# Windowed attention and a routed expert layer: score rows by (chunk, query), one product block a group, and another order of the eight-step pipeline

## The reference

```python
x = x + attention(layernorm_over_channels(x))   # 8x8 windows, 4 heads of 16, table bias
t = tokens(x)                                   # (4, 16384, 64)
t = t + experts(layernorm(t))                   # 8 experts, the best 2 of a softmax router
# attention, for each window and head:
attn = softmax(q @ k.T * hd**-0.5 + bias[rel_index])    # 64 x 64
out  = attn @ v ;  out = out @ w_proj.T + b_proj
# experts: sum over the two chosen e of p_e * (x @ W_e + b_e)
```

## Time and profile before

| what | value |
|---|---|
| median of 3 runs | 1214.26 us (1211.23 to 1214.93) |
| the profiled execution | 1211.91 us, span 1210.1 us |
| TensorE matmul busy | 1081.3 us, 89% |
| VectorE / ScalarE / GpSimd busy | 904.1 / 742.7 / 475.6 us (75 / 61 / 39%) |
| mean granted TensorE clock | 0.983 of full speed |

### The profile page before, as it was taken

One profiled execution on the slowest core, in us unless ns is written; L12 is line 12 of the kernel. 1 busy time (PEld: TensorE's weight loads), 2 busy tenths in 40 slices (PEclk: granted clock), 3 DMA queues, 4 the chain that ended last, 5 costly groups with the idle time before them and its releaser, 6 DMA issues.

```text
span 1210.1 us, 39081 instructions
## 1 busy us (share of the span) xinstructions
PE 1081.3 (89%) x16838; PEld 591.3 (49%) x16838; DVE 904.1 (75%) x1443; ACT 742.7 (61%) x1217; POOL 475.6 (39%) x421
## 2 busy tenths in 40 slices
PE   1688899999999999999999999999999999999653
PEld 1355455555555455555555555555555555554311
DVE  3246788888778788888778888888778888788552
ACT  0257767666766667666766667666766667665410
POOL 0001434444344434444344434444344434444443
PEclk9999999999999999999999999999999999999877
DMA  5000787666766887666667887666677887666667
GB/s 179 2 2 22 175 196 176 164 162 168 173 165 169 191 195 179 162 161 170 169 163 172 193 196 170 165 161 167 167 175 171 193 194 168 166 161 149 146 148 162
DMA packets 49255, 192.48 MB, mean 159 GB/s; under 512 B 10558, under 2 KB 10814, under 8 KB 32572
## 3 DMA queue, kind: packets, MB, share of 16 engines
q1 hardware_dynamic: 49084, 189.98, 65.6%
HBM read 154.04 MB, written 18.87 MB: 143 GB/s over the span
## 4 chain that ended last, share of the span: by engine, by line
PE 56%; DVE 19%; POOL 10%; ACT 7%; issue 3%; DMA 3%; SPq 1%; POOLq 0%; DVEq 0%; ACTq 0%
PE bank L594 10%; POOL tt L886 9%; PE bank L477 7%; PE bank L510 6%; PE bank L465 5%; PE bank L527 5%; PE bank L534 4%; PE bank L492 3%; DVE L L1109 3%; DVE ob L1067 3%; ACT prj L769 3%; PE bank L438 3%; ACT sq L775 3%; DVE Ls L1108 3%; PE bank L553 3%
## 5 line engine op out<-in xcount | busy, mean ns | idle before, releaser
L914 POOL TENSOR_TENSOR gz<-gz,tt 128x1024 f32<-128x1024 f32 x96 | 262.8, 2737 | 170.9 <-DMA gz<-gates_dram 170.9
L594 PE MATMUL bank<-gz,wex 64*64 64x512 f32 x2048 | 265.5, 614 | 16.2 <-DVE ob L1067 14.5
L886 POOL TENSOR_TENSOR tt<-prj,xs 128x512 f32<-128x512 f32 x64 | 109.1, 1727 | 369.1 <-ACT prj L769 369.1
L1036 DVE TENSOR_REDUCE mx<-bank 128x16 f32<-128x1024 f32 x128 | 156.1, 1220 | 106.5 <-PE bank L477 106.5
L1058 DVE TENSOR_TENSOR gz<-gz,tt 128x1024 f32<-128x1024 f32 x160 | 212.9, 1333 | 28.3 <-DMA gz<-gates_dram 28.3
L752 ACT ACTIVATE pt<-bank 128x512 f32<-128x512 f32 x256 | 151.2, 590 | 35.0 <-PE bank L510 34.2
L477 PE MATMUL bank<-km,qs 32*64 32x128 f32 x4096 | 172.5, 283 | 0.2
L510 PE MATMUL bank<-cst,probs 128*128 128x128 f32 x1024 | 167.5, 286 | 2.1 <-ACT pt L752 2.1
L1043 DVE TENSOR_TENSOR probs<-bank,mx 128x1024 f32<-128x1024 f32 x128 | 156.2, 1220 | 7.3 <-PE bank L510 1.8
L510 PEld LDWEIGHTS bank<-cst,probs 128*128 128x128 f32 x1024 | 110.3, 141 | 93.4 <-issue 58.9
L477 PEld LDWEIGHTS bank<-km,qs 32*64 32x64 f32 x4096 | 109.9, 132 | 67.1 <-issue 63.3
(11 more groups left out here) (111 smaller groups left out, 1432.1 us busy)
## 6 DMA issues: line engine op xcount, KB each, us to landing
gz<-gates_dram SPq DMA_DIRECT2D x256, 512.0 KB, 11.6
xs<-in_x SPq DMA_DIRECT2D x32, 512.0 KB, 16.3
tx<-tt SPq DMA_DIRECT2D x128, 128.0 KB, 3.9
out<-ob SPq DMA_DIRECT2D x128, 128.0 KB, 4.8
gz<-in_rel SPq DMA_DIRECT2D x1, 2048.0 KB, 9.4
gates_dram<-gt_rs SPq DMA_DIRECT2D x32, 64.0 KB
cst<-in_consts SPq DMA_DIRECT2D x1, 359.0 KB, 3.0
tt<-in_weights SPq DMA_DIRECT2D x4, 64.0 KB, 2.7
```

The lines of the kernel that those rows point to most:

```text
L594: last = mm(bank[64 * x:64 * x + 64, Y_BANK + a, :], wex[64 * a:64 * a + 64, e, :], gz[64 * a:64 * a + 64, s.pair(e)[1], e % 2, x * CH:(x ...
L886: tt_(chunk_windows(tt[s.buf(4)], x), as_windows(prj[:, x, :]), chunk_windows(xs[s.buf(4)], x), op=ALU.add).then_inc(t_ready, 1)
L914: tt_(gz[:, k, e % 2, :], gz[:, k, e % 2, :], tt[s.buf(4)][:, :], op=ALU.mult).then_inc(z_pool, 1)
L1036: red(mx[g % 2][:, :], two_banks(S_BANK).rearrange("p (c k) -> p c k", k=N), axis=AX_X, op=ALU.max).then_inc(max_done, 1)
```

## The change

It does four things.

1. Scores are laid out by (chunk, query) in the partitions; all four windows i of a group's chunk lie along the free dimension. The row tiles of chunk 0 write partitions 0 to 63 and those of chunk 1 partitions 64 to 127 of the same bank. `scores_left`, `scores_right` and `s_half` become one `scores`, with bias and all 16 products of a group in one block and no wait inside. `probs` and `pt` change shape to suit (the number and size of all instructions stay; `denominators` reads `pt` in runs of 64 elements in place of 128).
2. LAST_STAGE is 7: 39 steps. `project`, `move_proj`, `residual`, `square_residual` and `router` move from s3 to s4, most `experts` from s5 to s6 and the last three to s7, `finish` and `store` to s7, `swap_tokens` and the first three `spread_gates` to s5, and the loading and squaring of x to s0.
3. All five lists have another order.
4. `ROUNDS` is reordered to match.

```diff
-    LAST_STAGE = 6
+    LAST_STAGE = 7
...
-            0: [("lgT", 4, L_ready, 2), ("K", 2, k_ready, 2), ("Q", 2, q_ready, 1), ("stats", 1, var_done, 1),
-                ("gT", 4, gsb_ready, 2), ("V", 2, v_ready, 2), ("proj", 3, prj_ready, 1), ("spread", 1, xr_ready, 1)],
-            1: [("K", 2, k_ready, 2), ("Q", 2, q_ready, 1), ("V", 2, v_ready, 2), ("proj", 3, prj_ready, 1),
-                ("spread", 1, xr_ready, 1), ("router", 3, lg_ready, 1)],
+            0: [("proj", 4, prj_ready, 1), ("Q", 2, q_ready, 1), ("stats", 1, var_done, 1),
+                ("lgT", 4, L_ready, 2), ("K", 2, k_ready, 2), ("spread", 1, xr_ready, 1), ("gT", 4, gsb_ready, 2),
+                ("V", 2, v_ready, 2)],
+            1: [("proj", 4, prj_ready, 1), ("Q", 2, q_ready, 1), ("router", 4, lg_ready, 1), ("K", 2, k_ready, 2),
+                ("spread", 1, xr_ready, 1), ("V", 2, v_ready, 2)],
...
-                score_tiles(s, g, 0).then_inc(s_half, 1)
-
-            def scores_right(s, g):
-                pe.wait_ge(s_half, s.count(GROUPS, g + 1))
-                score_tiles(s, g, 1).then_inc(s_full, 1)
+                a = g // 2
+                for i in range(4):
+                    w = 4 * (g % 2) + i
+                    for r in range(4):
+                        x, hp = r // 2, r % 2
+                        last = mm(bank[N * x:N * x + N, S_BANK + hp, 128 * i:128 * i + 128],
+                                  qs[32 * r:32 * r + 32, a, w, :],
+                                  km[32 * r:32 * r + 32, CW * a + w, :, :].rearrange("p m k -> p (m k)"),
+                                  start=False, stop=(i == 3), skip_group_check=True)
+                last.then_inc(s_full, 1)
...
-                for r in range(4):
-                    last = nc.tensor.transpose(bank[:, PT_BANK, 128 * r:128 * r + 128],
-                                               probs[g % 2][:, r % 2, r // 2, u % 2, :], cv("ident"))
+                for j in range(2):
+                    for hp in range(2):
+                        at = 128 * (2 * j + hp)
+                        last = nc.tensor.transpose(bank[:, PT_BANK, at:at + 128],
+                                                   probs[g % 2][:, hp, 2 * (u % 2) + j, :], cv("ident"))
```

More of the change, by code:

```diff
@@ L602, in _ @@
                 if s[3].on:
-                    transposes(s[3], 3)
+                    transposes(s[3], 2)
+                if s[4].on:
+                    project(st, s[4])
+                if s[7].on:
+                    experts(s[7], 5)
+                    experts(s[7], 6)
+                if s[2].on:
+                    queries(st, s[2])
+                if s[3].on:
+                    transposes(s[3], 3)
+                if s[7].on:
+                    experts(s[7], 7)
+                if s[1].on:
+                    channel_sums(st, s[1])
+                if s[3].on:
+                    values(s[3], 0)
+                    values(s[3], 1)
+                if s[4].on:
+                    router(st, s[4])
+                if s[3].on:
+                    denominators(s[3], 0)
+                    transposes(s[3], 4)
                 if s[4].on:
@@ L606, in _ @@
                 if s[6].on:
[L607 removed]
+                    experts(s[6], 0)
                 if s[2].on:
@@ L1171, in _ @@
                 if s[1].on:
-                    guard_variance(s[1])
+                    split_std(s[1])
+                if s[4].on:
+                    gates(s[4])
                 if s[2].on:
                     row_max(s[2], 1)
+                    shift(s[2], 1)
+                if s[1].on:
+                    scale_x(s[1])
                 if s[3].on:
```

276 lines of the change are left out of this document (112 added, 164 removed).

## The result

The changed kernel takes **1203.93 us** (median of 4 runs, 1202.07 to 1205.98), the kernel before 1213.95 on the same chip: a ratio of 0.9918, with a 95% interval of 0.9896 to 0.9940. That is 0.8% faster where 3% was forecast. The time lies inside the range, near its slow end, but the forecast was wrong: less than a third of what was expected came. The profiled execution took 1205.98 us, its span was 1204.0.

The account below looks back on a forecast made before the run. TensorE's own list was taken as the bound. Step 31.7 + 0.4 + 1.1 = 33.2 us; span 1210.1 - 25 (steps) - 4 (fill) - 7 (drain) = 1174, plus 1.8 and 2.4: 1178 us, range 1141 to 1206.

Parts of the forecast that it names:

- The list: TensorE's own work per full step: 32.7 us falls to 31.7 (31.3 to 32.1) by eight fewer tile-shape changes.
- The block of a group: A group's scores on TensorE: two halves at 0.60 us each become one block of 1.03 us.
- rival C: In the scores block, row tiles of one bank take turns: 0.85 us more per group, step 36.6, 1273 us; chance 0.07.
- The new wait: Scores s2,0 wait 1.1 us a step for key copies behind token statistics, whose product GpSimd holds up.
- The waits on the normalise: TensorE's values waiting for normalise s3,0, 1.15 us a step before, were to go fully.
- the fill: Opening steps before the steady part: 4 us less, with 0 and 8 as ends.
- The router's wait of 0.4 us: TensorE reaches the router at 7.1 us, but the detour from project lets it start at 7.5.
- 33.2 us, 0.9 less. 28 x 0.9 = 25 us: Full step: 31.7 of list plus waits of 0.4 and 1.1, against 34.10 before, over 28 steps.
- Rival D: Thin covers give way, another wait at scores s2,1 or project: step 34.2 to 34.5, 1206 to 1214 us; chance 0.14.
- thin covers: Other meetings (scores s2,1 and s2,2, gates' transposes, values rows, project) found covered by only 0.2 to 0.8 us.
- rival B: GpSimd's lock delays the logits: keys wait for their copy, or logits start late; step 33.9, 1197 us; chance 0.17.
- the drain, "7 us less": From step 34's start: 24.7 us to last project, 21 to its gates' transposes, 32 to last VectorE instruction; 82 for 89.

Follow-up runs that it names:

- e2_keys_first: The changed kernel with the token variance's logarithm and root put behind the two key copies in ScalarE's list; 1178.56 us, ratio 0.9717.
- e1_after_thin: The changed kernel with each gate spread after the first six pairs cut to 16 of 64 partitions a half; 1162.78 us, ratio 0.9567.
- e7a_thin_late_pairs: The changed kernel with only the spreads of pairs 2 and 3 cut to 16 of 64 partitions a half; 1166.02 us, ratio 0.9599.
- e8: e2_keys_first with row_max and shift of s2,0 put ahead of top_two in VectorE's list; 1179.74 us, ratio 0.9715.
- x2: e8 with normalise s3,1 also put ahead of top_two in VectorE's list; 1180.26 us, ratio 0.9724.
- n1: The kernel before with the normalise of group 0 moved ahead of the logits and token choice in VectorE's list; 1212.07 us, ratio 0.9988.
- x1: e7a_thin_late_pairs with a DRAM-to-DRAM copy of the bytes left out behind each thinned pair 2 and 3; 1177.76 us, ratio 0.9708.

## Why the prediction was wrong, point by point

**Right.**
- The list: 33 stretches of one shape to 25 at 0.13 us each gave 31.7; 31.25 was measured. By that a change of shape costs 1.45 / 8 = 0.18 us, at the upper end of its bounds.
- The block of a group: 1.03 forecast, 1.04 measured. Row tiles of both chunks do run side by side in one bank, and rival C falls. The Trainium skill (TensorEngine Tiling (Array Packing), Restrictions and Gotchas) has different row tiles barred from one bank at the same time. By that the block would have taken 1.9 us, as an estimate, and the measurement decides: not so in different partition halves. The Trainium skill (PSUM — Partial Sum Buffer, PSUM bank collisions raise a hardware error) has different row tiles collide where they write one bank and the same 32-partition quadrant; the 1.04 us agree with that.
- The new wait: 1.1 us at scores s2,0 through the product held up by GpSimd, the statistics and the key copies behind them; 29.8 / 25 = 1.19 measured, the held-up product 1.92 us for 1.9, and e2_keys_first shows the last link, statistics ahead of the key copies, by cutting it.
- The waits on the normalise gone; the fill (-4.6 for -4).

**Too dear, by a little.** The router's wait of 0.4 us did not come. It was priced by the residual's 6.95 us detour of before, in which the two halves of `residual` took some 3.5 us beside VectorE's gating. In the new order they don't meet it:

```profile
570.25 2.53 POOL L872 TENSOR_TENSOR tt<-prj,xs 128x512 f32<-128x512 f32 x2 [7.01 <-ACT prj L758]
```

A duration taken from a row carries that row's neighbours with it.

**Wrong: "33.2 us, 0.9 less. 28 x 0.9 = 25 us".** The step that failed is the sum of a full step as list plus waits on semaphores. A quiet step was 32.2, 1.0 better still. The mean was 33.80: 1.60 more a step. Pauses make 33.6 / 27 = 1.24 of it. Of the other 0.36, some 0.19 is that the step shown is a good one: the nine of these 27 steps without any pause take 32.39 us on average. The two stretches at half clock make up to 2 x 3.41 / 2 / 27 = 0.13. By steps the books read: list -1.45, normalise and router waits -1.42, key wait +0.95, pauses and the rest +1.60, together -0.3, which is 33.80 - 34.10. The list and the waits were priced as meant; **the instructions' own way to TensorE had no term**, since the profile of before shows no such pause (0 of them). None of the rivals named it. Rival D came nearest in the time, with "another wait of 1 to 1.5 us takes the place of the old one", but at scores s2,1 or project by thin covers, and these covers held. That the time lies in the range at all is luck: rival B's step of 33.9 us is close to 33.80, but by keys that wait for the copy of the logits, and in the changed kernel they do not.

That the spreads cause the pauses is shown (e1_after_thin, e7a_thin_late_pairs); that they are late packets of TensorE's instructions is shown by the fixed count and by the packets' start times; that they grow as waits on semaphores are removed is shown from e2 to e8 to x2, though from the changed kernel to e2, where a wait moved to another block, they fell. Why the kernel before has none, with the same bytes moved, is shown in part. In its fast stretches, those of 256 records that TensorE ran through in under 6 us (pauses not counted), the packet due set out 0.45 us on average after TensorE passed the place, and at most 1.4 (24 stretches); in the changed kernel 2.1 and at most 6.0 (21 stretches). So the dense blocks of before lay where the DMA engines were free for the packets, and the new order put them beside spreads. The once-a-step wait for the normalise is not what held the pauses off, or only in small part: without it n1 has 5.0 us of them, against 33.6, though other waits had come in its place.

**Wrong: the drain, "7 us less".** It was 6.7 more, and these 13.7 us are nearly half of the 30 by which the span missed 1174. All three parts were too short by 3 to 5 us. The middle one took "that strip's first gates are spread ahead" for the end of waits on spreads; it came out at 26.3 us, 1.3 less than before, with a wait of 6.69 still in it. The last one was carried over from before with its 14.00 us wait. There the new wait of 12.40 ends 22.6 us after the gates' transposes, as it did before (22.2). What is longer stands behind it, 12.9 us for 10.0: five experts of the last strip run only after `finish` of the strip before, and in part at a low clock (0.65 on average from 1187.85 to 1194.70). No pause of the kind counted above lies behind 1080 us, so the drain is a matter of its own. This is read from the chains; no run tested it.

## What to carry to other kernels

Where a kernel's bound engine runs its list nearly without a gap and bulk transfers run beside it, a removed wait is not yet a gained microsecond: look whether blocks are cut in two with no semaphore between, and at which count of instructions; if the counts agree modulo a fixed number, as here, look at when the instruction queue's packets start: the supply of instructions may be the bound, and what helps then is to thin or move the transfers. Before crediting a change for a removed wait, thin the traffic in both kernels: here that alone showed that the new order and the new layout together were worth 0.16 us a step, and the transfers 1.2 to 1.3 us a step. And a small operation on a busy engine's list is moved ahead of a copy only after asking who waits for the copy: two ScalarE instructions of 0.2 us, put behind the key copies, gave 25 us.

## What the runs showed of the hardware that I had not expected

- TensorE pauses of 0.6 to 3.0 us with no semaphore behind them, each at the same place of a stretch of 256 instructions: 19 with 33.6 us in 880 us of the changed kernel, 1 with 0.6 us once pairs 2 and 3 are thinned. Each ended 2.5 to 3.1 us after the late start of a 16 KB packet of the instruction queue.
- They hang on where and what the transfers are, not only on their load: DMA engines 91% busy at 249 GB/s, copies added in the old order, gave 3.5 us of pauses, and spreads of the same bytes as the copies of x1 gave about five times its 6.8 us.
- After a pause of 2.8 us the granted clock was 0.57 over the next four microseconds, so that this pause cost more than its own length; of the 19 pauses two were followed by such a stretch.
- The profile's label "issue" stood for such a pause and for a plain wait on ScalarE's key copies alike. The place tells them apart: one comes at the same block in every step, the other at a count of instructions and in the middle of a block.
